# ScalarE takes the ratio exponentials straight from the input; VectorE bounds them afterwards and bounds the reciprocal

## The reference, cut to what matters

```python
ek = jnp.exp(jnp.minimum(kf, 30.0))
ekv = ek * vf
# nf, df: a = a * decay + ekv_t, b = b * decay + ek_t, forward in time; nb, db: the same backward
euk = jnp.exp(jnp.minimum(u.astype(jnp.float32)[None, None, :] + kf, 30.0))
num = nf + nb - ekv + euk * vf
den = df + db - ek + euk
base = jax.nn.sigmoid(r.astype(jnp.float32)) * (num / jnp.maximum(den, 1e-08))
out = base * (0.8 + 0.2 * tf)
```

## Time and profile before

| what | value |
|---|---|
| median of 3 runs | 3973.22 us (3966.16 to 3978.81) |
| the profiled execution | 3973.28 us |
| its span on the core | 3971.5 us |
| PE busy | 3450.7 us (87%) |
| DVE busy | 2610.3 us (66%) |
| ACT busy | 1180.8 us (30%) |
| POOL busy | 503.4 us (13%) |
| mean granted TensorE clock | 0.914 |

### The profile page before, as it was taken

One profiled execution on the slowest core, in us unless ns is written; L12 is line 12 of the kernel. 1 busy time (PEld: TensorE's weight loads), 2 busy tenths in 40 slices (PEclk: granted clock), 3 DMA queues, 4 the chain that ended last, 5 costly groups with the idle time before them and its releaser, 6 DMA issues.

```text
span 3971.5 us, 37643 instructions
## 1 busy us (share of the span) xinstructions
PE 3450.7 (87%) x12941; PEld 2128.7 (54%) x12941; DVE 2610.3 (66%) x3732; ACT 1180.8 (30%) x1948; POOL 503.4 (13%) x404
## 2 busy tenths in 40 slices
PE   1877878878879999999999589998989898989998
PEld 0553553553555776777777346543554356434643
DVE  5877877877875777888888244664466435644563
ACT  1332332332331544333433132212222223123210
POOL 1002003003003111111111201110212011201100
PEclk9979989989989999999999797899789978998799
DMA  3202201201203878788787500231013201220011
GB/s 137 80 28 46 80 30 46 81 29 34 73 29 123 274 239 262 228 272 264 254 277 242 219 37 1 85 120 65 32 75 111 85 32 75 100 97 32 2 63 42
DMA packets 276638, 436.71 MB, mean 110 GB/s; under 512 B 52320, under 2 KB 189536, under 8 KB 263904
## 3 DMA queue, kind: packets, MB, share of 16 engines
q1 hardware_dynamic: 256768, 379.84, 28.9%
q0 software_dynamic: 19680, 54.46, 4.2%
HBM read 364.59 MB, written 93.77 MB: 115 GB/s over the span
## 4 chain that ended last, share of the span: by engine, by line
PE 61%; DVE 23%; DVEq 6%; ACT 4%; issue 2%; DMA 2%; POOL 1%; SPq 0%; ACTq 0%; POOLq 0%
PE bank L1012 11%; PE bank L1041 6%; PE bank L1283 6%; PE bank L1296 4%; PE bank L1304 4%; PE bank L1212 4%; PE bank L828 3%; PE bank L1149 3%; DVE sb_gla L1884 3%; PE bank L1190 2%; DVE sb_ratio L1859 2%; DVEq L1865 2%; PE bank L1018 2%; PE bank L1248 1%; PE bank L808 1%
## 5 line engine op out<-in xcount | busy, mean ns | idle before, releaser
L1012 PE MATMUL bank<-sb_xT,sb_work 128*128 128x256 f32 x2304 | 513.0, 382 | 1.6 <-issue 0.8
L1012 PEld LDWEIGHTS bank<-sb_xT,sb_work 128*128 128x128 f32 x2304 | 439.3, 192 | 75.2 <-issue 17.5
L828 PE MATMUL bank<-sb_gla,sb_work 128*128 128x256 f32 x896 | 260.3, 443 | 112.6 <-DVE sb_work L1886 100.0
L1041 PE MATMUL bank<-sb_work,sb_hT 128*128 128x512 f32 (+1 forms) x666 | 296.1, 592 | 0.0
L828 PEld LDWEIGHTS bank<-sb_gla,sb_work 128*128 128x128 f32 x896 | 188.9, 218 | 175.6 <-DVE sb_work L1886 121.1
L808 PE MATMUL bank<-sb_hT,sb_work 128*128 128x512 f32 x384 | 181.1, 620 | 99.6 <-DVE sb_hT L1833 99.6
L1296 PE MATMUL bank<-sb_parts,sb_gla 128*128 128x512 f32 x512 | 240.3, 613 | 4.5 <-ACT sb_gla L1628 4.5
L1304 PE MATMUL bank<-sb_parts,sb_gla 128*128 128x512 f32 x512 | 230.8, 593 | 5.9 <-DVE sb_work L2450 5.9
L1283 PE MATMUL bank<-sb_work,sb_parts 128*128 128x512 f32 x512 | 230.8, 610 | 2.8 <-ACT sb_work L1641 2.8
L1884 DVE TENSOR_TENSOR sb_gla<-sb_gla,sb_work 128x1024 f32<-128x1024 f32 x112 | 146.0, 1303 | 128.9 <-PE bank L828 122.9
L1149 PE MATMUL bank<-sb_parts,sb_hT 128*128 128x512 f32 x512 | 228.7, 605 | 0.0
(11 more groups left out here) (396 smaller groups left out, 6103.3 us busy)
## 6 DMA issues: line engine op xcount, KB each, us to landing
sb_work<-scratch_gu SPq DMA_DIRECT2D x63, 1408.0 KB, 7.5
sb_parts<-scratch_mx SPq DMA_DIRECT2D x16, 3072.0 KB, 12.1
sb_work<-moe_w SPq DMA_DIRECT2D x63, 512.0 KB, 6.7
scratch_y<-sb_work SPq DMA_DIRECT2D x48, 512.0 KB, 7.8
sb_parts<-scratch_fq SPq DMA_DIRECT2D x24, 1024.0 KB, 8.0
sb_work<-w_qkvg SPq DMA_DIRECT2D x64, 256.0 KB, 2.5
scratch_gu<-moe_w SPq DMA_DIRECT2D x32, 512.0 KB, 5.8
sb_parts<-fT SPq DMA_DIRECT2D x48, 256.0 KB, 3.4
```

The source lines that it names most:

```text
L828: mm = pe.matmul(dst.rearrange("p (h n l) -> p h n l", h=HPC, l=size), kS[u % 2][:, k * P:(k + 1) * P], late[:, :, k, :, 1, :], start=True ...
L1012: mm = pe.matmul(dst, egu[j % 3][:, which * NC + k, m * P:(m + 1) * P], xt[j % 2][:, k, :], start=(k == 0), stop=(k == NC - 1))
L1041: mm = pe.matmul(bank(YB[s]), einter[j % 2][0:n, a:a + P], edn[j % 3][0:n, m * D:(m + 1) * D], start=(m == 0), stop=(m == EC - 1))
```

## The change

ScalarE no longer waits for VectorE's `min(f, 30)` and `min(f + u, 30)`: it reads the input itself, and takes `u` as the bias of the second exponential. VectorE bounds the exponentials by exp(30) when it takes them over (`bounded_products`), just ahead of the product with f, which now also carries the factor `oscale` (it stood in the quotient). `ek` is bounded and multiplied in piece 0, `euk` only behind the scans, in piece 2. The bound 1e-8 below the denominator becomes a bound 1e8 above its reciprocal, inside the quotient. The scans move by half a piece: piece 0 ends with the first forward scan, pieces 1 and 2 hold the other three. New counters tell ScalarE when the scans have read `ekp` (`r_scan`) and when the quotient has read `eup` (`r_half`, `r_done`), so the first exponential of a unit may run while the unit before is still in pieces 3 to 5. The two buffers for the bounded inputs go. The order of all steps on every engine stays.

```diff
--- before.py
+++ after.py
@@ -250,8 +250,8 @@
         N1 = 2 * NB * NC
         NPAIR = N1 + NB * NC
         ld_f = [ev(f"ld_f{i}", 1, 16) for i in range(2)]
-        r_min, r_min2, r_done = series("r_dve", 3)
-        r_exp, r_exp2 = series("r_act", 2)
+        r_half, r_scan, r_done = series("r_dve", 3)
+        r_ek, r_eu, r_eu2 = series("r_act", 3)
         st_r = [ev(f"st_r{i}", 1, 32) for i in range(2)]
 
         sig0 = ev("sig0", NC)
@@ -429,7 +429,6 @@
 
         ekp, eup = (R[2][:, i * 1024:(i + 1) * 1024] for i in range(2))
         nf2, nb2 = (R[3][:, i * 1024:(i + 1) * 1024] for i in range(2))
-        fmin_e, fmin_u = small2[:, 4 * T:5 * T], w(16896, T)
         fch = [big[:, 11264 + s * T:11264 + (s + 1) * T] for s in range(2)]
 
 
@@ -1319,13 +1318,20 @@
 
         def ratio_exps(act, m, second):
 
+            _, g0, c = unit_of(m)
             if second:
-                act.wait_ge(r_min2.sem, r_min2.at(m, 1))
-                act.activation(eup[:, T:2 * T], fmin_u, ACT.Exp).then_inc(r_exp2.sem, 1)
+                act.wait_ge(r_half.sem, r_half.at(m, 1))
+                act.activation(eup[:, T:2 * T], fch[m % 2], ACT.Exp, bias=wu4[:, g0 + 1, 1, c:c + 1])\
+                   .then_inc(r_eu2.sem, 1)
             else:
-                act.wait_ge(r_min.sem, r_min.at(m, 1))
-                act.activation(ekp[:, T:2 * T], fmin_e, ACT.Exp)
-                act.activation(eup[:, T:2 * T], fmin_u, ACT.Exp).then_inc(r_exp.sem, 1)
+                act.wait_ge(ld_f[m % 2].sem, 16 * (m // 2 + 1))
+                if m:
+                    act.wait_ge(r_scan.sem, r_scan.at(m - 1, 1))
+                act.activation(ekp[:, T:2 * T], fch[m % 2], ACT.Exp).then_inc(r_ek.sem, 1)
+                if m:
+                    act.wait_ge(r_done.sem, r_done.at(m - 1, 1))
+                act.activation(eup[:, T:2 * T], fch[m % 2], ACT.Exp, bias=wu4[:, g0, 1, c:c + 1])\
+                   .then_inc(r_eu.sem, 2 if m < N1 else 1)
 
 
         @block.scalar
@@ -1349,9 +1355,7 @@
 
             def exps(m):
 
-                act.wait_ge(r_min.sem, r_min.at(m, 1))
-                act.activation(ekp[:, T:2 * T], fmin_e, ACT.Exp)
-                act.activation(eup[:, T:2 * T], fmin_u, ACT.Exp).then_inc(r_exp.sem, 2)
+                ratio_exps(act, m, False)
 
             exps(0)
             sigmoids0(0)
@@ -1774,56 +1778,54 @@
             dve.tensor_copy(base, cst("ebase"))
             dve.drain()
 
-            def ratio_start(m):
-
-                _, g0, c = unit_of(m)
-                f = fch[m % 2]
-                dve.wait_ge(ld_f[m % 2].sem, 16 * (m // 2 + 1))
-                ts(fmin_e, f, 30.0, None, ALU.min)
-                ts(fmin_u, f, wu4[:, g0, 1, c:c + 1], 30.0, ALU.add, ALU.min).then_inc(r_min.sem, 1)
+            E30 = float(np.exp(30.0))
+
+            def bounded_products(pair, m):
+
+                b = unit_of(m)[0]
+                ts(pair[:, T:2 * T], pair[:, T:2 * T], E30, None, ALU.min)
+                dve.drain()
+                stt(out=pair[:, 0:T], in0=pair[:, T:2 * T], scalar=oscale[:, b:b + 1], in1=fch[m % 2],
+                    op0=ALU.mult, op1=ALU.mult)
+
+            def quotient(g, c):
+
+                return stt(out=ch(R[g], c), in0=nb2[:, 0:T], scalar=1e8, in1=eup[:, 0:T], op0=ALU.min, op1=ALU.mult)
 
             def ratio_step(r):
 
                 m, step = N1 + r // 6, r % 6
                 b, g0, c = unit_of(m)
-                g, f = g0 + step // 3, fch[m % 2]
+                g = g0 + step // 3
                 dk = decay3[:, b, g * NC + c:g * NC + c + 1]
                 if step % 3 == 0:
 
-                    done = r_exp if step == 0 else r_exp2
-                    dve.wait_ge(done.sem, done.at(m, 1))
                     if step == 0:
-                        tt(ekp[:, 0:T], ekp[:, T:2 * T], f, ALU.mult)
-                    tt(eup[:, 0:T], eup[:, T:2 * T], f, ALU.mult)
-                    dve.drain()
+                        dve.wait_ge(r_ek.sem, r_ek.at(m, 1))
+                        bounded_products(ekp, m)
+                        dve.drain()
                     for a in range(2):
                         src = ekp[:, a * T:(a + 1) * T]
                         dve.tensor_tensor_scan(nf2[:, a * T:(a + 1) * T], dk.to_broadcast([P, T]), src, 0.0,
                                                ALU.mult, ALU.add)
-                        dve.tensor_tensor_scan(nb2[:, a * T:(a + 1) * T][:, ::-1], dk.to_broadcast([P, T]),
-                                               src[:, ::-1], 0.0, ALU.mult, ALU.add)
+                        q = dve.tensor_tensor_scan(nb2[:, a * T:(a + 1) * T][:, ::-1], dk.to_broadcast([P, T]),
+                                                   src[:, ::-1], 0.0, ALU.mult, ALU.add)
+                    if step:
+                        q.then_inc(r_scan.sem, 1)
+                    eu = r_eu2 if step else r_eu
+                    dve.wait_ge(eu.sem, eu.at(m, 1))
+                    bounded_products(eup, m)
                 elif step % 3 == 1:
                     nf, nb = r3(nf2, T)[:, :, 0:T - 1], r3(nb2, T)[:, :, 1:T]
                     stt(out=nf, in0=nb, scalar=dk, in1=nf, op0=ALU.mult, op1=ALU.add)
                     dve.drain()
                     tt(eup, eup, nf2, ALU.add)
-                    dve.drain()
-                    ts(eup[:, T:2 * T], eup[:, T:2 * T], 1e-8, None, ALU.max)
                 else:
                     dve.reciprocal(nb2[:, 0:T], eup[:, T:2 * T])
                     dve.drain()
                     if m >= N1 + NC and step == 2:
                         dve.wait_ge(st_r[m % 2].sem, 32 * ((m - N1 - NC) // 2 + 1))
-                    q = stt(out=ch(R[g % 2], c), in0=eup[:, 0:T], scalar=oscale[:, b:b + 1], in1=nb2[:, 0:T],
-                            op0=ALU.mult, op1=ALU.mult)
-                    if step == 5:
-                        q.then_inc(r_done.sem, 1)
-                        if m + 1 < NPAIR:
-                            dve.drain()
-                            ratio_start(m + 1)
-                    else:
-                        dve.drain()
-                        ts(fmin_u, f, wu4[:, g0 + 1, 1, c:c + 1], 30.0, ALU.add, ALU.min).then_inc(r_min2.sem, 1)
+                    quotient(g % 2, c).then_inc((r_done if step == 5 else r_half).sem, 1)
                 dve.drain()
 
             def gate0(b):
@@ -1838,33 +1840,40 @@
                 m, piece = divmod(n, 6)
                 b, g, c = unit_of(m)
                 dk = decay3[:, b, g * NC + c:g * NC + c + 1]
+
+                def forward(a):
+                    half = slice(a * T, (a + 1) * T)
+                    dve.tensor_tensor_scan(nf2[:, half], dk.to_broadcast([P, T]), ekp[:, half], 0.0,
+                                           ALU.mult, ALU.add)
+
+                def backward(a):
+                    half = slice(a * T, (a + 1) * T)
+                    return dve.tensor_tensor_scan(nb2[:, half][:, ::-1], dk.to_broadcast([P, T]),
+                                                  ekp[:, half][:, ::-1], 0.0, ALU.mult, ALU.add)
+
                 if piece == 0:
-                    dve.wait_ge(r_exp.sem, r_exp.at(m, 1))
-                    tt(ekp[:, 0:T], ekp[:, T:2 * T], fch[m % 2], ALU.mult)
-                    tt(eup[:, 0:T], eup[:, T:2 * T], fch[m % 2], ALU.mult)
-                elif piece <= 2:
-                    half = slice((piece - 1) * T, piece * T)
-                    src = ekp[:, half]
-                    dve.tensor_tensor_scan(nf2[:, half], dk.to_broadcast([P, T]), src, 0.0, ALU.mult, ALU.add)
-                    dve.tensor_tensor_scan(nb2[:, half][:, ::-1], dk.to_broadcast([P, T]), src[:, ::-1], 0.0,
-                                           ALU.mult, ALU.add)
+                    dve.wait_ge(r_ek.sem, r_ek.at(m, 1))
+                    bounded_products(ekp, m)
+                    dve.drain()
+                    forward(0)
+                elif piece == 1:
+                    backward(0)
+                    forward(1)
+                elif piece == 2:
+                    backward(1).then_inc(r_scan.sem, 2)
+                    dve.wait_ge(r_eu.sem, r_eu.at(m, 1))
+                    bounded_products(eup, m)
                 elif piece == 3:
                     nf, nb = r3(nf2, T)[:, :, 0:T - 1], r3(nb2, T)[:, :, 1:T]
                     stt(out=nf, in0=nb, scalar=dk, in1=nf, op0=ALU.mult, op1=ALU.add)
                     dve.drain()
                     tt(eup, eup, nf2, ALU.add)
                 elif piece == 4:
-                    ts(eup[:, T:2 * T], eup[:, T:2 * T], 1e-8, None, ALU.max)
-                    dve.drain()
                     dve.reciprocal(nb2[:, 0:T], eup[:, T:2 * T])
                 else:
-                    stt(out=ch(R[g], c), in0=eup[:, 0:T], scalar=oscale[:, b:b + 1], in1=nb2[:, 0:T],
-                        op0=ALU.mult, op1=ALU.mult).then_inc(r_done.sem, 2)
-                    dve.drain()
-                    ratio_start(m + 1)
-                dve.drain()
-
```

(4 more changed lines are left out.)

## The result

The changed kernel takes **3962.55 us** (median of 14 runs, 3959.23 to 3969.48) against 3974.53 us (14 runs) for the kernel before beside it: ratio **0.9974, 95% interval 0.9966 to 0.9982**. Forecast were 3957.7 us and a gain of 15.6; measured is a gain of 12.0, with 7 to 13.5 inside the interval, so the change is faster beyond noise and the gain is somewhat smaller than forecast. The profiled execution has a span of 3957.6 us, 13.9 less than the 3971.5 of before.

A forecast was written before the change was run, and what follows sets the result against it. TensorE was 61% of the chain of waits, VectorE with its queue 29%, taking turns in attention and routing. Start -5.0, attention +1.2, routing -7.9, experts -3.9: -15.6 from 3973.28, giving 3957.7 us, range 3947 to 3968.

The forecast's parts named there:

- Start, -5.0: Before the first `gate0`: earlier first product (-1.37) and three handovers (-1.19 each) save 5.0 us.
- Attention, +1.2: Attention of four batches: longer piece 0 against shorter pieces 4 and 5, 1.2 us slower in sum; bounds -3 to +20.
- +1.26: Piece 0 grows from 1.37 to 2.63 us; in chunk 0 of batches 0 and 3 fully on the path.
- Rival 3: Slower: longer piece 0 exposed in all 16 attention chunks, new GpSimd meetings in 12; +12.8 us, 3986.1; chance 0.06.
- Routing, -3.1 per batch: Routing, batches 0 to 2: handovers and shorter pieces outweigh longer pieces 0, 3.1 us saved per batch; -7.9 for three.
- Batch 0, -1.7: Routing of batch 0: the last unit's input lands 0.96 late, so only about 1.7 us is saved.
- ScalarE now meets that wait: VectorE can start at about 363.9: Last unit of batch 0's routing: ScalarE takes the late input's wait; VectorE starts there instead of 365.29, gaining 1.4 us.
- Experts, -3.9: Expert stage: TensorE's two waits ended by `prep_out` shrink by 0.2 and 3.7 us; bounds 0 and -12.1.
- The other tiles have slack of some tenths either way: 0: Expert stage, tiles outside the two priced waits: no gain or loss.
- Rival 1: Expert stage refills: its two waits end by something unmoved, a table load slips behind `r_scan`; -10.4 us, 3962.9; chance 0.20.
- Rival 2: Both of TensorE's waits in the expert stage go entirely; 8.2 us more gain, 3949.5; chance 0.10.
- The port rule: VectorE and GpSimd lock shared ports per instruction; added bounds may meet GpSimd products, 0.78 us seen; as many meetings expected after.

The follow-up runs named there:

- exp_before_xt: Changed kernel with ScalarE's expert-stage order altered: exponentials heading a tile ahead of `expert_xt`, others behind the first `prep_out`; 3940.72 us, ratio 0.9922; repeat 3941.15, 0.9907.
- before_xt: Kernel before the change, with only ScalarE's new order of ratio exponentials, `expert_xt` and `prep_out` in the expert stage; 3951.90 us, ratio 0.9938.
- pieces_old: Changed kernel with the old pieces, exponentials and bounds at the start, in attention and in routing, new steps only in the experts; 3969.90 us, ratio 0.9980.

## Why the prediction was right, and where not

**Start, -5.0: right** (-5.07). Each price held: bound 0.51, product 0.83, no idle time ahead of piece 0. But only half of it came through at first. TensorE's windows behind `gate0`, before and after:

```profile
81.00:104.00 23.00, 19.34 (x67) 1.00 0.40 126
```

```profile
76.00:101.00 25.00, 21.41 (x65) 0.90 0.42 138
```

TensorE kept 2.4 GHz through this stretch before. After, it had 1.2 GHz from about 96 on, behind 3 us without a matmul, and took 2.1 us more for the same kind of work. The same kernel shows both (`exp_before_xt` took 24.09 us from the first `gate0` to the first level at a granted clock of 1.00, its repeat 26.17 at 0.91), and 26.1 stands once with the old pieces too, so the change is not needed for it; whether it makes it more frequent, these few profiles don't say. The prediction had no term for it.

**Attention, +1.2: right in kind by chunks, but the sum owes its closeness to the clock.** The whole is -0.6 (+0.1 without batch 0). By chunks, over batches 1 to 3: chunk 0 +0.5, +0.9 and +0.6 (0.5, 0.5 and 1.26 forecast), chunk 1 +0.4, +0.3, +0.1 (0.8 each), chunk 2 +0.1, +0.2, -0.1 (-0.2), chunk 3 -1.2, -1.1, -0.7 (-1.2). Piece 0 in chunk 0 of batch 3, which I put fully on the path, reads so after, for the earlier trace rows:

```profile
994.74 0.43 DVE L1786 TENSOR_SCALAR sb_ratio<-sb_ratio 128x512 f32<-128x512 f32 x1
995.24 0.75 DVE L1788 SCALAR_TENSOR_TENSOR sb_ratio<-sb_ratio,sb_small,sb_parts 128x512 f32<-128x512 f32 x1
996.07 1.23 DVE L1846 TENSOR_TENSOR_SCAN sb_ratio<-sb_small,sb_ratio 128x512 f32<-128x512 f32 x1
997.37 1.23 DVE L1893 TENSOR_TENSOR sb_gla<-sb_gla,sb_work 128x1024 f32<-128x1024 f32 x1
```

It lasts 2.63, as priced, and the level starts at once. The 1.26 was indeed paid there: first to second level takes 6.99 where it took 5.72. But from third to fourth level it is 7.53 after 5.70 (a meeting with GpSimd that had been one level later), and then 5.62 after 6.46, 5.15 after 5.65 and 3.80 after 4.97: +3.1 and -2.5. Of the -2.5, 0.8 is that meeting gone from its old place and 0.5 is the shorter piece 4, which I had put at 0. The last 1.2 is not the change's: the kernel before took 3.65 there in batches 1 and 2, and 4.97 in batches 0 and 3, the latter at a granted clock of 0.84 over these two levels (0.97 after), and in `before_xt`, the same code up to the experts, batch 0 has the 3.65. Without this stretch in batches 0 and 3 attention would have come out near +2. The step that was wrong is "+1.26" in batches 0 and 3: I followed it to the next level and not to the end of the chunk. Rival 3 (every piece 0 exposed, attention over 16.8) is out.

**Routing, -3.1 per batch: right for batches 1 and 2** (-3.12 and -3.61). The wait ahead of L2157 is 2.76 where 3.12 stood, and the handovers have no idle time. **Batch 0, -1.7: wrong** (+2.2 and, in the second profile, +2.5). The step that failed is "ScalarE now meets that wait: VectorE can start at about 363.9". VectorE did start earlier than that, at 360.38, but I took the lateness of the load for a fixed date and the rest of the stage as free of it. (The sum is wrong as well: with 1.4 in place of the 2.03 of one handover, -3.1 becomes -2.5 and not -1.7.) The lateness belongs to the 24 scatters, as the run without them shows, and moves with the issue of the load; and in both profiles of the change a second stall of 3.3 to 4.1 us, whose cause is open, meets VectorE at L2157. With the old pieces, in `pieces_old` and `before_xt`, the same input kept VectorE 3.09 and 3.40 us where it was 0.96 in the profile I had, and batch 0's routing took 130.5 and 130.8 us. So 0.96 was a lucky price, and the +2.2 is measured against a lucky 127.17: over all profiles the new pieces are not seen to make batch 0 slower. A wait of one row, for a transfer beside other transfers, should have had a range. Of the prediction's signs of being wrong, one came true here: VectorE waits for `r_ek`, 2.88 us, once.

**Experts, -3.9: right in mechanism, missized** (-6.67). The first wait went from 5.76 to 5.61 (-0.2 forecast), the second from 6.35 to 2.63 (-3.7 forecast, 2.6 left: exact). What I left out are two smaller waits of the trace before, ended by `round_blocks`:

```profile
1665.68 0.66 PE L1050 MATMUL bank<-sb_const,sb_parts 128*128 128x128 f32 x4 [1.16 <-DVE sb_parts L2212]
...
1682.50 0.66 PE L1050 MATMUL bank<-sb_const,sb_parts 128*128 128x128 f32 x4 [0.22 <-DVE sb_parts L2212]
```

They are gone after: 1.4. The period of four tiles went from 60.54 to 60.46, nine times: 0.7. With 0.15 and 3.72 this makes 6.0; 0.7 is not placed. "The other tiles have slack of some tenths either way: 0" is the step that failed: VectorE's slack, once gained, passed on to the next waits. Rival 1 (the stage refills) is out, and of its table load behind `r_scan`, which did come, no one had to wait. Rival 2 (both waits go) was 5 us too hopeful for the change, but right about what could be had: another order took both.

**The port rule.** In the changed kernel a bound in chunk 0 of batch 3 took 1.42 us beside a GpSimd product, 0.40 without:

```profile
1008.47 1.87 POOL L1672 TENSOR_TENSOR sb_gla<-sb_work 128x512 f32<-128x512 f32 x1 [1.79 <-PE bank L853]
```

```profile
1009.20 1.42 DVE L1786 TENSOR_SCALAR sb_ratio<-sb_ratio 128x512 f32<-128x512 f32 x1
```

It is the same meeting as in the earlier trace rows, at 1.02 instead of 0.78. The Trainium skill (SBUF — State Buffer, Who interferes with whom) has tensor_scalar in its two-port mode among those that contend with GpSimd for the shared ports, and also every instruction with two inputs in SBUF, as the scan has. The trace agrees for both: the bound above, and a scan of 2.18 us beside a product at 1084.57, 1.20 alone. In the earlier trace rows the product still had 0.90 us to run when the scan began, so its 0.78 is near a full wait and not exactly one. I had counted as many meetings as before; among the ratio instructions there are nine, 8.1 us of stretching, where there had been six and 4.2. That is far from rival 3's twelve new ones.

In the sum, +3.9 (batch 0) and +2.45 (clock) stood against -2.8 (experts), -1.8 (attention) and small ones, and the total came out 1.7 us above the forecast in the profile and 3.6 in the median of the first runs. It was right partly because misses cancelled, and the -1.8 of attention is itself the clock's. The forecast gain of 15.6 lies outside the interval of 7 to 13.5. Rival 1 named a time nearer to the median than the forecast did, but for a reason that the stages refute: the experts gave 6.7 us, and no wait of TensorE for L1049 there grew by more than 0.1.

## What to carry to other kernels

A handover between two engines is won by starting the other engine's work from the point where its buffer comes free, not by making either engine's work smaller: here nearly the same work, started one step earlier, is worth 12 us. Before moving a wait, look where the table load will stand: with one wait put back behind the quotient the program was 32 us slower than the change and 21 slower than the kernel before, with the loads behind it too. When a trace shows an engine waiting for a short instruction that queues behind a longer one on a third engine, look first at the order on that third engine: two moved calls gave 19 to 22 us in their stage, more than the change in the whole kernel. Price a transfer that lies beside scatters from more than one row, and follow VectorE's gained slack through all later waits of the stage, also the small ones.

## What was not expected of the hardware

- A transfer of 256 KB beside GpSimd's 24 scatters was usable 19.4 to 23.1 us after its issue in batch 0 and landed after 12 to 16.5 us in batch 1 and 9 to 12.8 in batch 2; away from the scatters it landed after 2.5 to 2.8. Weights came 12 us late in chunk 1 when the scatters were moved there.
- The granted clock of TensorE falls in different places in executions of the same program: 2.1 us behind a `gate0` (1.00 and 0.91) and 2.7 us between two levels (0.97 and 0.69). Between two programs with the same code behind the experts it made 8 us (0.76 and 0.79). An edit that changes nothing there can seem to gain or lose as much.
- The quotient with a number as its scalar and a minimum as its first operation takes 0.69 us, with a column of 128 values and a product 0.75. Which of the two differences counts is not shown.
- Where the first exponential has two waits ahead of it (for its input and for the scans), its table load of 1.28 us ran behind the wait for the scans: 12 loads started only when the scans were done. One of them, at 348.88, ran while the input was still awaited. With a single wait, in the kernel before, the loads ran ahead of it.
